# One more tile's value product on VectorE, and scatters ahead of a GpSimd product, in a per-token head-mixing stage

## The reference

```
q, k, v = (xn @ W).reshape(tokens, H, HD)          # H = 16 heads, HD = 8
s = einsum('nhd,ntd->nht', q, k) * HD ** -0.5      # 16 x 16 per token
p = softmax(s, axis=-1)
x = x + einsum('nht,ntd->nhd', p, v).reshape(tokens, D) @ Wfc
xn = (x - mean(x)) / sqrt(var(x) + 1e-5)
logits = xn @ router_w.T                           # 8 experts; the top two are taken
```

## Time and profile before

| | us |
|---|---|
| median of 3 runs | 3168.54 (3162.38 to 3168.88) |
| the profiled execution | 3168.54, its span 3166.8 |
| PE busy | 2356.6 (74%) |
| VectorE busy | 2087.7 (66%) |
| ScalarE busy | 1458.0 (46%) |
| GpSimd busy | 918.6 (29%) |

### The profile page before, as it was taken

One profiled execution on the slowest core, in us unless ns is written; L12 is line 12 of the kernel. 1 busy time (PEld: TensorE's weight loads), 2 busy tenths in 40 slices (PEclk: granted clock), 3 DMA queues, 4 the chain that ended last, 5 costly groups with the idle time before them and its releaser, 6 DMA issues. The chain is left out here.

```text
span 3166.8 us, 45213 instructions
## 1 busy us (share of the span) xinstructions
PE 2356.6 (74%) x13976; PEld 1471.9 (46%) x13976; DVE 2087.7 (66%) x5228; ACT 1458.0 (46%) x3105; POOL 918.6 (29%) x968
## 2 busy tenths in 40 slices
PE   2397688849857699999999976579574955577774
PEld 2397577749834222222222234479364954122223
DVE  3455667745554899999999924445674565487775
ACT  1265211116542378888888852156323653133222
POOL 4544245544410000100100003534264431121220
PEclk9999789869978789999999988689686976798997
DMA  4122000002212400000000000012111220000000
GB/s 141 41 66 76 27 8 14 14 25 62 70 40 93 159 14 19 19 19 19 17 19 19 9 29 21 32 53 65 60 34 43 66 87 0 23 0 0 0 0 27
DMA packets 118265, 121.56 MB, mean 38 GB/s; under 512 B 21936, under 2 KB 101520, under 8 KB 117264
## 3 DMA queue, kind: packets, MB, share of 16 engines
q1 hardware_dynamic: 98720, 72.85, 8.0%
q0 software_dynamic: 17840, 40.55, 3.8%
q10 hardware_dynamic: 1472, 5.26, 0.5%
HBM read 67.21 MB, written 50.99 MB: 37 GB/s over the span
## 5 line engine op out<-in xcount | busy, mean ns | idle before, releaser
L1709 DVE TENSOR_REDUCE attn_mx<-bank 128x1 f32<-128x512 f32 x1024 | 640.9, 682 | 60.5 <-PE bank L1488 52.1
L1610 ACT ACTIVATE attn_pT<-bank 128x512 f32<-128x512 f32 x1024 | 539.9, 603 | 125.9 <-PE bank L1503 125.5
L1488 PE MATMUL bank<-attn_K,attn_Q 48*128 48x512 bf16 x1024 | 335.9, 395 | 48.1 <-DVE attn_mx L1709 29.3
L1503 PE MATMUL bank<-attn_Q,attn_K 51*128 51x512 bf16 x1024 | 330.4, 385 | 2.8 <-ACT attn_pT L1610 1.6
L1516 PE MATMUL bank<-attn_pT,attn_vb 128*32 128x512 f32 x2048 | 275.3, 609 | 20.0 <-ACT attn_pT L1610 11.7
L1669 POOL TENSOR_TENSOR attn_m_rem<-attn_m_rem,attn_m_parts 8x128 f32<-8x128 f32 x128 | 53.4, 417 | 683.5 <-ACT attn_m_parts L1623 683.5
L1488 PEld LDWEIGHTS bank<-attn_K,attn_Q 48*128 48x128 bf16 x1024 | 71.8, 94 | 372.3 <-DVE attn_mx L1709 322.6
L2357 POOL TENSOR_TENSOR mix_rS<-mix_rT,mix_S 128x512 f32<-128x512 f32 x64 | 81.6, 1279 | 292.9 <-ACT mix_gT L2337 233.7
L891 PE MATMUL bank<-mix_prod_qk,ident 128*128 128x256 f32 x512 | 125.6, 402 | 0.0
L1000 POOL TENSOR_TENSOR mix_prod_pv<-mix_prob,mix_kv 128x2048 f32<-128x2048 f32 x24 | 97.6, 4068 | 90.8 <-ACT mix_prob L958 90.8
L891 PEld LDWEIGHTS bank<-mix_prod_qk,ident 128*128 128x128 f32 x512 | 104.3, 205 | 26.4 <-issue 12.0
(11 more groups left out here) (605 smaller groups left out, 5813.3 us busy)
## 6 DMA issues: line engine op xcount, KB each, us to landing
attn_q_parts<-attn_rope_q_parts SPq DMA_DIRECT2D x48, 128.0 KB, 2.0
attn_k_parts<-attn_rope_k_parts SPq DMA_DIRECT2D x48, 128.0 KB, 2.0
attn_Q<-attn_q_parts SPq DMA_DIRECT2D x64, 96.0 KB
attn_K<-attn_k_parts SPq DMA_DIRECT2D x64, 96.0 KB
ffn0a_x_ring<-xs_rows SPq DMA_DIRECT2D x72, 64.5 KB
ffn0b_x_ring<-xs_rows SPq DMA_DIRECT2D x72, 64.5 KB
ffn2a_x_ring<-xs_rows SPq DMA_DIRECT2D x72, 64.5 KB
ffn2b_x_ring<-xs_rows SPq DMA_DIRECT2D x72, 64.5 KB
```

What stands on the lines that cost most here:

```text
L1488: nc.tensor.matmul(a_bank[n % 3][:], slot(net.Q, h, 0, KROWS)[:, qt * P:(qt + 1) * P], slot(net.K, h, 0, KROWS)[:, hf * CH:(hf + 1) * CH], ...
L1503: nc.tensor.matmul(s_bank[n % 3][:], slot(net.K, h, 0, KROWS + MROWS)[:, kt * P:(kt + 1) * P], slot(net.Q, h, 0, KROWS + MROWS)[:, hf * CH ...
L1610: nc.scalar.activation(pT[:, kt % RING, hf * CH:(hf + 1) * CH], s_bank[(n * HPB + hf) % 3][:], ACT.Exp, scale=HD ** -0.5).then_inc(exp_rea ...
L1709: nc.vector.tensor_reduce(mx[:, h % 2, qt, hf:hf + 1], a_bank[n % 3][:], AX.X, ALU.max).then_inc(a_used, 1)
```

## The change

Three things. Place 1 of each chunk leaves `SUMMED`: its value product goes from GpSimd to VectorE and its sum from TensorE to VectorE. On TensorE the logits at place 2 stand behind that tile's `sum_values` and no more ahead of it. On GpSimd the eight scatters are cut into two groups of four, one ahead of the last product of the chunk and one behind it.

```
-        HH, KV, QK, SUMMED = H * H, 8, 3, (0, 1, 2)
+        HH, KV, QK, SUMMED = H * H, 8, 3, (0, 2)
...
                 if after == 2:
                     pe.wait_ge(y_added, c)
                     norm.turn(pe, c - 1)
-                    norm.logits(pe, c - 1, router.rw)
                 if n >= 0 and is_summed(n):
                     sum_values(n)
+                if after == 2:
+                    norm.logits(pe, c - 1, router.rw)
...
                 if c > 0:
                     norm.rstd_pow(pool, c - 1)
+                if c > 1:
+                    norm.scatter(pool, c - 2, (0, 1))
                 times_values(c * TPC + SUMMED[1])
-                times_values(c * TPC + SUMMED[2])
                 if c > 1:
-                    norm.scatter(pool, c - 2)
+                    norm.scatter(pool, c - 2, (2, 3))
```

## The result

The changed kernel takes 3221.54 us (median of 4 runs, 3219.49 to 3229.88) against 3168.71 for the kernel before in the same comparison: ratio 1.0174, 95% interval 1.0149 to 1.0198. Measured again beside 20 runs of the kernel before, it takes 3221.41 against 3174.39: 1.0150 (1.0118 to 1.0183). So it is 47 to 53 us slower; the forecast was +61.1, 3229.6 us, in a range of 3206 to 3250.

A forecast was written before the change was run, and what follows sets the result against it. The prediction took a loop between TensorE and VectorE in stage mix as the bound. Its terms, 40.7 + 12.8 + 11.7 - 0.6 - 3.5 = +61.1 us on 3168.54, gave 3229.6 us, range 3206 to 3250.

The forecast's parts named there:

- Steps 2 and 3: VectorE gains tile 1's product and reduction, 4.87 us, and loses L314's stall, 3.70: pos moves by +1.17 us.
- Step 4: GpSimd's product for tile 2 stands behind four scatters waiting for pos: it ends at 578.16 instead of 567.10 us.
- rounds 2 to 6: Stretches between turnings of the mixed tiles (L909): rounds 2, 3, 5, 6 together +40.7 us, round 4 +12.8.
- Step 6: TensorE's clock is low after 7 us idle in mid-round: sum 6.3 us, logits 1.5, copy +10.17.
- its start loses the luck that it had: Round 4, before 2.58 us shorter than round 5, gets the usual slow start; with +10.17 together +12.8 us.
- Round 7: Last round of stage mix: copy of the logits +14.0 us, less an earlier wait of 2.33, gives +11.7.
- round 1: Round without scatters, so the product isn't held: -0.6 us, bounds -3.6 and 0.
- Chunk 0: Ahead of round 1, where TensorE has the say: a sum of 3.57 us leaves, -3.5, bounds -3.6 and +1.3.
- Rounds of 48 to 53 us: Sign of the forecast in rounds 2 to 6; 45 to 48 us with sums at 3.65 would show full clock.
- Full clock: Rival, chance 0.18: mid-round restart costs nothing and round 4 keeps its start; +7.12 us a round, +40, 3208.6.
- Clock lower still: Rival, chance 0.16: sum and logits wholly at 1.2 GHz, first scores slow to the end; +81, 3249.7 us.
- The other side: Rival, chance 0.04: GpSimd's product isn't held and the scatters are free; -10 us, 3158.5.

The follow-up runs named there:

- e1: The changed kernel run again with no edit; 3221.41 us, ratio 1.0150 to the kernel before.
- e2: The changed kernel with all eight scatters behind GpSimd's last product; 3176.73 us, ratio 1.0003 to the kernel before.
- e5: The changed kernel with all eight scatters ahead of GpSimd's last product instead of four; 3258.23 us, ratio 1.0269 to the kernel before.
- e7: The kernel before with only the scatters cut, four ahead of tile 2's product and four behind; 3175.34 us, ratio 1.0009.
- e3: The changed kernel with the logits ahead of tile 2's sum again; 3172.18 us, ratio 0.9985 to the kernel before.
- e9: The changed kernel with 14 filler matmuls on TensorE ahead of tile 2's sum; 3215.87 us, ratio 1.0135 to the kernel before.
- e4: The changed kernel with the edits of e2 and e3 together, leaving only tile 1's move to VectorE; 3151.01 us, ratio 0.9931 to the kernel before.
- e11: e4 repeated without further edit; 3149.85 us, ratio 0.9923 to the kernel before.
- e6: The changed kernel with 28 filler matmuls on TensorE ahead of tile 2's sum; 3248.09 us, ratio 1.0238 to the kernel before.

## Why the prediction was right, and what was mis-sized

- **The forecast as a whole.** 3229.6 us in a range of 3206 to 3250; measured 3221.54 and 3221.41, inside. The path and the order of the waits are the predicted ones. But the 8 us of the miss flatter it: the stage came to +44.7 (+43.2 in e1) where +61.1 was forecast, and the 10 us by which other stages were longer than in before's trace brought the sum nearer. That part is luck.
- **What bounds the kernel.** Right. From the copy of the logits to the next turning is 613.96 - 602.28 = 11.68 us, forecast 11.69.
- **Steps 2 and 3.** The pair to its scale takes 583.68 - 579.01 = 4.67 us (4.66), the scale holds 0.20 (0.21), L314 is 0.19. The placing's last operation, pos, starts at the turning + 19.46. Forecast was + 21.96 with the slow start of 2.6 us that this round didn't have; without it 19.4.
- **Step 4, on which the sign rests.** From pos to the end of the product: 595.03 - 585.64 = 9.39 us, forecast 578.16 - 568.79 = 9.37. TensorE's wait is 6.79 (about 7). e2 takes the hold away and gets 45 us back; e5 adds 5.06 us of hold and the wait grows by 5.04. It is shown, and so is its condition: when the logits don't stand behind the held product, its hold leaves rounds 2 to 6 as they were in the kernel before (e7), and with the pair on VectorE it costs some 28 instead of 45 us, in part through VectorE's stall on L261 (e3).
- **Step 6.** The sum took 6.20 us (6.3), from its start to the copy 7.20 (7.8): the logits ran at the full clock again. Six rounds times 0.6 is 3.6 us too much.
- **The start of the rounds is the term that was mis-sized.** I kept the slow start in rounds 3, 5 and 6 and added one to round 4, "its start loses the luck that it had". In all four the clock rose earlier instead: project and first scores ran at 1.16 and 3.62 us (round 5 above; the earlier trace rows had 5.32). That is 3 x 2.6 + 2.6 = 10.4 us. I took it that a longer idle gap leaves at least the usual slow start behind it. With gaps of 6.27 us the start was fast in the changed kernel (8.24 us to the first sum) and slow in e9 and e2 (10.81, 10.97), and round 2 of the changed kernel, behind a gap of 6.45 us both times, started slow in the first trace and fast in e1. So the gap's length alone doesn't tell, and what does stays open.
- **The other terms.** Round 7 came to +11.2 (+11.7), round 1 to -0.95 (-0.6). Chunk 0, from the first projection to the first turning, came to 39.61 - 45.50 = -5.9 us in the first trace and -4.3 in e1: both beyond the bound of -3.6 on the forecast's -3.5. What gave the rest stays open.
- Put together: rounds 2 to 6 were forecast at +53.5 and measured +40.3 (+37.2 in e1); with round 7, round 1 and chunk 0 the stage's +61.1 came to +44.7 (+43.2).
- **The signs.** L900's wait of 6.79 us, L272's of 12.77, L314 at 0.19 eight times and 512 instructions of L900 came as said. Two did not. Rounds of 48 to 53 us were the sign: only round 2 of the first trace was (50.35), the others took 47.4 to 47.8, which is the length named for the full clock, but with sums of 6.2 us and not of 3.65. And the second product of a round starts 8.6 us later in its round, not some 11, because the fast start moved all behind it.
- **The rivals.** "Full clock" (+40) is nearest to the stage's +44.7, but by another way than it says: the restart in mid-round did cost 2.5 us, and the round's start returned as much. That its +7.12 us a round is so near to the measured +7.13 of round 5 is two errors that cancel. "Clock lower still" didn't occur. "The other side" gave -10 us for a version whose product isn't held: e2 is that version, at -0.2 us at the last turning. Most of the difference is round 7, +3.8 us instead of -2.9, and round 4, which lost its fast start (+2.8 instead of -0.6).
- The rule of the Trainium skill's "TensorE: Matmul & The Clock Gate", section "What's actually happening", that for modelling the ramp's loss is under 1% of a typical kernel's span, is borne out for the one slow stretch that step 6 priced: 2.5 us in six rounds is 15 of 3221 us, 0.5%. What the low clock costs in the rest of the program wasn't summed. Here 1% would be 32 us, most of the effect.

## What to carry to other kernels

In these traces each engine ran its instructions in the order in which they were written: the product stood behind a scatter's wait of 11.64 us. So before a wait is moved ahead of other work, look at what stands behind it and who waits for that in turn. Four cheap scatters here carried that wait to a product, a sum and a choice of experts on three engines. The same edit was free, but for one round, where its product was not needed soon (e7), cost some 28 us beside the moved tile (e3 against e4 and e11), and 45 us together with two others (e2 against the changed kernel), so edits that share a chain are priced together. A stall too has to be priced by where it falls: worth nothing beside a wait (L314 in the kernel before), and on one of the two longest paths when the product was moved (L261 in e3). And taking them apart paid: of the three, the moved tile alone makes the kernel 0.7 to 0.8% faster (e4, e11).

## What the runs showed of the hardware

- In a loop with idle gaps, the stretch at the low clock moved about: rounds kept their length when it went from the sum (6.20 us, start at + 8.24) to the start (3.68 us, + 10.81). Filling one gap gained 2.8 us in a stage of 360 (e9).
- The start of the same round of the same kernel, behind the same gap, can be slow in one execution and fast in the next: round 2 of the changed kernel took 50.35 and 47.42 us.
- A small VectorE product of two SBUF operands took 3.89 us beside a GpSimd product and 0.19 without; in e3 another took 4.55, ending (571.51) with the GpSimd product (571.45). In e7 the stall was gone from all rounds and the length of rounds 2 to 6 stayed within 0.03 us: a stall of nearly twenty times the operation's own length, worth nothing there.
- An indirect DMA issued from GpSimd holds it 0.96 us and 0.30 of issue each; four ahead of a product delayed it by 590.98 - 586.10 = 4.88 us.
- A float32 matmul of 256 columns takes 0.43 us at the full clock (28 in 12.1, e6), recorded as two instructions.
